# Cross attention on one core: SyncE issues the three k parts of a stack after the values and the first half of the rows

## The chip, the cores and the metric

The kernel runs on one NeuronCore of a Trainium2 chip. The metric is the device time of one execution in microseconds (us). Five engines work side by side: TensorE (PE, with its weight loads shown as PEld), VectorE (DVE), ScalarE (ACT), GpSimd (POOL) and SyncE (SP). SP computes nothing; it issues nearly all DMAs of this kernel, in the order of its program, and it waits on semaphores between them.

## The reference

A cross attention with 16 batches of 256 queries, 256 keys, width 320 and 20 heads of 16. The last 8 keys are 4 "dummy" and 4 "ip" tokens with their own weights, their own softmax and a mask built from boxes:

```python
q = split_heads(x @ w_q)                       # (16, 20, 256, 16)
k, v = split_heads(text @ w_k), split_heads(text @ w_v)       # 248 keys
out_text = softmax(q @ k.T / 4) @ v
k_ip, v_ip = split_heads(ip_h @ w_k_ip), split_heads(ip_h @ w_v_ip)   # 8 keys
out_ip = softmax(q @ k_ip.T / 4 + mask_ip) @ v_ip
out = (out_text + out_ip) @ w_out + b_out + x
```

All of it is float32. The kernel splits operands into high and low parts to keep the accuracy in TensorE's faster float format.

## The kernel before

**First stage** (about the first 210 us): eight groups of two batches each project q, k and v, split q and k into high and low parts, and write them to DRAM (`q_parts`, `k_parts`, `v_rows`).

**Second stage**: 16 batches, one after the other, each with 10 pairs of heads. `batches` runs batches 0 and 1 written out, then a hardware loop of two rounds over six batches (2 to 7, 8 to 13), then 14 and 15. What matters here is how a batch b uses what SP brings:

- A **stack** is what the scores of one batch need: q rows and k rows of all heads, interleaved over the partitions in four kinds of rows. Kinds 0 to 2 are q parts (`load_q`) or k parts (`load_k`), kind 3 of q is the mask (`load_aux`). There are three stacks in turn (w = batch modulo 3). A stack takes seven DMAs of 320 KB, all on the semaphore `stack_loaded[w]`.
- In batch b TensorE computes for each pair p `key_scores(b, p)` (L716, transposed scores that ScalarE turns into `probs` with an exponential, L471) and right behind it `query_scores(b + 1, p)` (L666, scores of the NEXT batch, from which VectorE takes the row maxima, L534 and L536). `values` (L730) and the output projection (L739) follow in between. `query_scores(b + 1, 0)` waits for the whole stack of b + 1, all seven DMAs (L654). So the stack b + 2, which SP issues during batch b, is asked for by the second group of matmuls of batch b + 1.
- **Rows**: the maxima of batch b + 1 go into row 31 of the q stack of b + 1. When VectorE has the maxima of five pairs, it turns them (`turn`, L542) into `row_buf`; SP writes them to DRAM (`store_rows`, L227), waits until they have landed (L229) and reads them back into the stack (`load_rows`, L232). `key_scores(b + 1, 0)` waits for the rows of the first half (h = 0, L712), `key_scores(b + 1, 5)` for those of the second.
- **Values**: `load_values` (L297, L299) brings 660 KB for batch b + 1; it may start once `values` of batch b - 1 are done, that is shortly after batch b begins.

TensorE's order within a batch is fixed by hand, and each wait in it holds everything behind it. So is SP's order, which is the function `batch` of the sync block. In it `scored(t, 0)` waits until key scores of batch b - 1 are done, so that the stack b + 2 may take the place of b - 1; at that point of the program the wait has long been fulfilled.

Of the kernel before, what the change touches and what calls it, by code (L numbers as in the profile page):

```python
# [29 lines left out]
def xattn(nc, x, xT, ctxT, ctx_sp, bbox, wq, wk, wv, wk_ip, wv_ip, wo, bias, grid, kaux, vones, out):  # L30
# [12 lines left out]
    with ctx:  # L43
# [106 lines left out]
        def need(eng, s, value):  # L150
            if not isinstance(value, int) or value > 0:
                eng.wait_ge(s, value)
# [11 lines left out]
        def rows_of(stack, kind):  # L164
            return stack[kind::KINDS, :].rearrange("p (a n) -> p a n", a=PAIRS).bitcast(f32)
# [28 lines left out]
        def _(sp):  # L194
# [30 lines left out]
            def store_rows(b, h):  # L225
                sp.wait_ge(rows_turned, 2 * b + h + 1)
                sp.dma_start(max_rows[h].rearrange("r (t i n) -> i r t n", t=2, i=4),  # L227
                             row_buf[:, h, :].rearrange("p (t n) -> p t n", t=2)).then_inc(rows_stored, 16)
            def load_rows(t, h):  # L229
                sp.wait_ge(rows_stored, 16 * (2 * t.b + h + 1))  # L230
                dst = q_stacks[t.w][2 * DH - 1::2 * DH, h * HALF * S:(h + 1) * HALF * S]
                sp.dma_start(dst.rearrange("p (a n) -> p a n", a=HALF).bitcast(f32),  # L232
                             max_rows[h][0:4 * HALF, :].rearrange("(a x) n -> x a n", x=4)).then_inc(rows_loaded[h], 16)
# [42 lines left out]
            def load_q(t, j):  # L276
                src = q_parts[j // 2, :, bass.ds(t.b * S, S)].rearrange("(a er) n -> er a n", a=PAIRS)
                sp.dma_start(rows_of(q_stacks[t.w], j), src).then_inc(stack_loaded[t.w], 16)  # L278
            def load_aux(t):
                src = aux_rows[bass.ds(t.b, 1), :, :].rearrange("a r n -> (a r) n")  # L280
                sp.dma_start(rows_of(q_stacks[t.w], KINDS - 1),
                             src.unsqueeze(1).broadcast_to([2 * DH, PAIRS, S])).then_inc(stack_loaded[t.w], 16)
            def load_k(t, j):
                src = k_parts[j % 2, :, bass.ds(t.b * KEYS, KEYS)].rearrange("(a er) n -> er a n", a=PAIRS)
                sp.dma_start(rows_of(k_stacks[t.w], j), src).then_inc(stack_loaded[t.w], 16)  # L285
            def load_stack(t):
                for j in range(3):
                    load_q(t, j)
                load_aux(t)
                for j in range(3):  # L290
                    load_k(t, j)
# [4 lines left out]
            def load_values(b, u):  # L296
                sp.dma_start(v_cur[:, u, 0:2, :], v_rows[bass.ds(b, 1), :, :, :].rearrange(  # L297
                    "a k p n -> (a p) k n")).then_inc(v_loaded[u], 16)
                sp.dma_start(v_cur[P - NSP:P, u, 2, :], v_sp_rows[bass.ds(b, 1), :, :].rearrange(  # L299
                    "a p n -> (a p) n")).then_inc(v_loaded[u], 16)  # L300
            def load_residual(b, u):
                sp.dma_start(x_res[:, u, :, :], rows(x[bass.ds(b * S, S), :])).then_inc(xr_loaded[u], 16)
# [12 lines left out]
            def scored(t, p):  # L315
                need(sp, st_ready, PAIRS * t.b + p)
            def batch(t):
                b, u = t.b, t.u
                ahead, next_, first = t.there(2), t.there(1), isinstance(b, int) and b == 0
                if not first:  # L320
                    load_rows(t, 1)
                if t.there(-2):
                    store_out(b - 2)
                load_residual(b, u)
                if ahead:
                    scored(t, 0)
                    load_stack(t.to(2))
                if next_:
                    need(sp, pv_ready, QUADS * b)
                    load_values(b + 1, 1 - u)  # L330
                    store_rows(b + 1, 0)
                    load_rows(t.to(1), 0)
                    store_rows(b + 1, 1)
            def store_out(b):
                need(sp, out_done, OT * (b + 1))
                sp.dma_start(rows(out[bass.ds(b * S, S), :]), out_sb[:, :, :]).then_inc(out_stored, 16)
            batches(sp, batch, tail=False)
            for b in (B - 2, B - 1):
                store_out(b)
# [473 lines left out]
```

## Time and profile before

| | |
|---|---|
| median of 3 runs | 558.0 us (553.15 to 563.45) |
| the profiled execution, device time | 556.4 us |
| its span (first to last instruction) | 554.6 us |
| PE busy, DVE busy, ACT busy | 87%, 69%, 51% of the span |
| second stage, batches 0 to 15 | from 211.8 us to the end |
| data moved | 112.49 MB, mean 203 GB/s |

The span is 1.8 us shorter than the device time of that execution. Matmuls are pipelined and their ends are modelled, so that a busy PE is not PE at its peak; what counts below are the distances between starts.

### The profile page before, as it was taken

The numbers are of one execution on the slowest core, as the hardware profiler recorded it, in microseconds if no ns is written. First come the engines' busy times: TensorE is split into PE (matmuls) and PEld (weight loads), VectorE is DVE, ScalarE is ACT, GpSimd is POOL, SyncE is SP. The second block draws the span as 40 slices with busy tenths as digits, with TensorE's granted clock in tenths as the row PEclk, the third lists the DMA queues.
The fourth block names the chain that finished last, engine by engine and source line by source line (L and its number), as shares of the span: only waits on it lengthen the run. The fifth ranks groups of instructions, "written<-read, shape, count | busy, mean of one in ns | idle before, by whom it ended". The sixth has DMA issues, their size and how long they took to land.

```text
span 554.6 us, 12517 instructions
## 1 busy us (share of the span) xinstructions
PE 481.5 (87%) x4304; PEld 323.7 (58%) x4304; DVE 384.9 (69%) x706; ACT 280.3 (51%) x355; POOL 127.9 (23%) x205
## 2 busy tenths in 40 slices
PE   3979899999999586799799889897987988989985
PEld 2868687887887463455455555554554555555542
DVE  2739425325325256899779989897997999999932
ACT  3633335344344013666556666565664666666671
POOL 6014000000000000432323332331332433332341
PEclk9989999999999787999979999999998999999999
DMA  8978888888788935672681762672754654763211
GB/s 271 362 266 149 259 298 273 309 268 293 272 261 270 345 120 179 200 243 74 204 261 33 247 221 89 234 233 79 235 170 154 219 154 144 245 204 103 72 52 47
DMA packets 94195, 112.49 MB, mean 203 GB/s; under 512 B 14304, under 2 KB 72992, under 8 KB 94144
## 3 DMA queue, kind: packets, MB, share of 16 engines
q1 hardware_dynamic: 93296, 109.89, 60.6%
q0 software_dynamic: 848, 1.90, 1.9%
q8 instruction: 33, 0.54, 0.4%
q14 instruction: 18, 0.15, 0.1%
HBM read 73.17 MB, written 38.63 MB: 202 GB/s over the span
## 4 chain that ended last, share of the span: by engine, by line
PE 48%; DMA 15%; issue 11%; SPq 10%; DVE 9%; ACT 4%; POOL 3%; DVEq 0%; ACTq 0%; POOLq 0%
PE pv L730 10%; DMA max_rows<-row_buf 10%; PE score_t L716 5%; PE pj L739 4%; PE score_q L666 3%; ACT probs L471 3%; SPq L278 3%; PE score_t L625 3%; PE score_t L626 3%; PE score_t L627 3%; SPq L285 2%; PE pj L625 2%; DMA q_stack<-max_rows 2%; PE pj L627 2%; PE pj L626 2%
## 5 line engine op out<-in xcount | busy, mean ns | idle before, releaser
L534 DVE TENSOR_REDUCE max_cols<-score_q 128x4 fp32r<-128x992 f32 x160 | 187.1, 1170 | 46.4 <-PE score_q L666 41.1
L471 ACT ACTIVATE probs<-score_t 128x1024 f32<-128x1024 f32 x160 | 163.4, 1021 | 72.0 <-PE score_t L716 71.9
L730 PE MATMUL pv<-probs,v_cur 128*32 128x256 f32 x1920 | 124.5, 394 | 0.6 <-ACT probs L471 0.6
L387 POOL TENSOR_TENSOR o_turned<-o_turned,inv_cols 128x256 f32<-128x256 f32 x80 | 49.8, 622 | 179.7 <-DVE inv_cols L589 179.7
L716 PE MATMUL score_t<-q_stack,k_stack 64*128 64x256 f32 x440 | 56.5, 335 | 29.4 <-ACT probs L471 17.6
L730 PEld LDWEIGHTS pv<-probs,v_cur 128*32 128x32 f32 x1920 | 55.3, 111 | 41.1 <-issue 4.6
L462 ACT ACTIVATE o_all<-pv 128x512 f32<-128x512 f32 x80 | 47.8, 598 | 60.7 <-PE pv L730 60.7
L716 PEld LDWEIGHTS score_t<-q_stack,k_stack 64*128 64x128 f32 x440 | 33.8, 189 | 74.8 <-ACT probs L471 37.7
L739 PE MATMUL pj<-wo_sb,o_all 128*128 128x320 f32 x192 | 69.0, 468 | 2.9 <-DVE o_all L594 2.2
L381 POOL TENSOR_TENSOR x_all<-x_all,bias_sb 128x640 f32<-128x640 f32 x16 | 24.9, 1554 | 192.5 <-DMA x_all<-in_x 192.5
L586 DVE STREAM_TRANSPOSE o_turned<-o_all 128x512 f32<-128x512 f32 x80 | 56.1, 702 | 11.9 <-ACT o_all L462 11.9
L666 PE MATMUL score_q<-k_stack,q_stack 64*128 64x256 f32 x440 | 47.2, 293 | 12.1 <-DVE max_cols L536 7.0
L513 DVE TENSOR_TENSOR stack<-o_all,stack 128x1024 fp32r<-128x1024 f32 x16 | 19.0, 1222 | 54.3 <-ACT stack L406 54.3
L666 PEld LDWEIGHTS score_q<-k_stack,q_stack 64*128 64x128 f32 x440 | 35.7, 195 | 15.0 <-DVE max_cols L536 6.9
L739 PEld LDWEIGHTS pj<-wo_sb,o_all 128*128 128x128 f32 x192 | 31.1, 188 | 18.7 <-DVE o_all L594 3.9
L392 POOL TENSOR_TENSOR o_all<-o_turned 128x128 f32<-128x128 f32 x80 | 36.7, 459 | 9.3 <-POOL o_turned L387 5.5
L716 PE MATMUL score_t<-stack 64*128 64x256 f32 x200 | 25.2, 330 | 10.6 <-ACT probs L471 7.0
L716 PEld LDWEIGHTS score_t<-stack 64*128 64x128 f32 x200 | 15.0, 184 | 31.3 <-ACT probs L471 16.1
L536 DVE TENSOR_REDUCE max_cols<-score_q 128x4 fp32r<-128x32 f32 x160 | 28.8, 180 | 0.0
L417 ACT ACTIVATE qk_out<-score_t 128x512 fp32r<-128x512 f32 (+1 forms) x24 | 13.9, 593 | 24.8 <-PE score_t L627 14.4
L625 PE MATMUL pj<-stack,wk_hl 128*128 128x512 f32 x32 | 13.8, 430 | 11.4 <-DVE stack L513 11.4
L525 DVE TENSOR_TENSOR qk_out<-score_t,qk_out 128x512 fp32r<-128x512 f32 (+1 forms) x24 | 15.8, 681 | 9.6 <-ACT qk_out L417 9.6
(134 smaller groups left out, 719.5 us busy)
## 6 DMA issues: line engine op xcount, KB each, us to landing
q_stack<-q_parts SPq DMA_DIRECT2D x33, 320.0 KB, 4.5
k_stack<-k_parts SPq DMA_DIRECT2D x33, 320.0 KB, 5.6
v_rows<-v_out SPq DMA_DIRECT2D x32, 320.0 KB, 2.4
v_cur<-v_rows SPq DMA_DIRECT2D x16, 640.0 KB
o_all<-in_ctxT SPq DMA_DIRECT2D x16, 512.0 KB, 5.2
q_parts<-qk_out SPq DMA_DIRECT2D x32, 256.0 KB, 2.5
k_parts<-qk_out SPq DMA_DIRECT2D x32, 248.0 KB, 4.7
x_all<-in_x SPq DMA_DIRECT2D x16, 320.0 KB, 3.3
```

Source lines behind the costliest of these rows:

```text
L387: pool.tensor_tensor(out, out, inv_cols[:, k, :].unsqueeze(2).broadcast_to([P, 2 * S // 32, DH]), ALU.mult).then_inc(scaled, 1)
L392: pool.tensor_tensor(o_norm_t[:, k // 2, :, half:half + DH], out[:, 0:S // 32, :], out[:, S // 32:, :], ALU.add).then_inc(o_added, 1)
L462: nc.scalar.activation(o_raw[:, k, :], pv[:, :], ACT.Copy)\
L471: nc.scalar.activation(probs[:, slot(u, p), :], score_t[:, :], ACT.Exp, scale=SCALE)\
L534: nc.vector.tensor_reduce(out=max_cols[:, h, :, at:at + 4:2].rearrange("p t e -> p e t"), in_=both[:, :, :, 0:TEXT], op=ALU.max, axis=AX.X ...
L536: nc.vector.tensor_reduce(out=max_cols[:, h, :, at + 1:at + 4:2].rearrange("p t e -> p e t"), in_=both[:, :, :, TEXT:KEYS], op=ALU.max, ax ...
L586: nc.vector.transpose(turned_blocks(k), o_raw[:, k, :].rearrange("p (j n) -> p j n", n=32))\
L625: mm(out, w_hi, x_hi_, start=start, stop=False)
L666: last = mm(score_bank(first, p, e)[:, tile * KEYS:(tile + 1) * KEYS], q_cols(w, p, e, tile * P, P), k_cols(w, p, e, 0, KEYS), start=True, ...
L716: last = mm(score_t[:, 512 * e + S * tile:512 * e + S * tile + S], k_cols(t.w, p, e, tile * P, P), q_cols(t.w, p, e, 0, S), start=True, st ...
L730: last = mm(pv[32 * t:32 * t + 32, at:at + S], values_of(u, kind, 4 * k + t), probs[:, slot(u, 2 * k + t // 2), a:a + S], start=kind != 1, ...
L739: last = mm(pj[:, 0:D], o_norm[:, u, c, t * P:t * P + P], wo_sb[:, c, :], start=c == 0, stop=c == OC - 1)
```

## The change

In SP's program of a batch, `load_stack` is taken apart. q and mask of the stack b + 2 keep their place. The three k parts are issued after the values of b + 1, after the store of the first half of the rows and after their load, which itself waits for the landing of the store. The store of the second half stays last. No DMA is added or removed, and no semaphore changes.

```diff
                 if ahead:
                     scored(t, 0)
-                    load_stack(t.to(2))
+                    for j in range(3):
+                        load_q(t.to(2), j)
+                    load_aux(t.to(2))
                 if next_:
                     need(sp, pv_ready, QUADS * b)
                     load_values(b + 1, 1 - u)
                     store_rows(b + 1, 0)
                     load_rows(t.to(1), 0)
+                if ahead:
+                    for j in range(3):
+                        load_k(t.to(2), j)
+                if next_:
                     store_rows(b + 1, 1)
```

## Rows read from the trace of the kernel before

**Rows 1.** The page, the chain that ended last, shares of the span by line

```profile
PE pv L730 10%; DMA max_rows<-row_buf 10%; PE score_t L716 5%; PE pj L739 4%; PE score_q L666 3%; ACT probs L471 3%; SPq L278 3%; PE score_t L625 3%; PE score_t L626 3%; PE score_t L627 3%; SPq L285 2%; PE pj L625 2%; DMA q_stack<-max_rows 2%; PE pj L627 2%; PE pj L626 2%
```

**Rows 2.** Waits of the whole span: us in total, times, longest

```profile
PE score_t L716 <- DMA q_stack<-max_rows: 11.8, 7, 3.2
...
PE score_t L716 <- DMA stack<-max_rows: 1.4, 1, 1.4
```

**Rows 3.** Windows from one batch's first key scores to the next's (batches 3, 4, 5, 6, 10)

```profile
276.00:298.31 22.31, 20.93 (x212) 11.90 (x213) 17.49 (x33) 12.79 (x15) 5.83 (x9) 0.85 0.52 168
298.31:319.04 20.73, 18.10 (x212) 10.69 (x212) 19.64 (x41) 12.69 (x15) 6.93 (x11) 1.00 0.57 182
319.04:338.73 19.69, 18.12 (x212) 10.72 (x213) 17.71 (x35) 12.68 (x15) 6.96 (x11) 1.00 0.58 191
338.73:359.94 21.21, 18.09 (x213) 10.70 (x213) 19.86 (x42) 12.68 (x15) 6.92 (x11) 1.00 0.55 178
...
423.88:445.06 21.18, 19.65 (x213) 11.22 (x213) 17.47 (x33) 12.68 (x15) 6.59 (x11) 0.92 0.54 177
```

The columns are: the window, its length, busy us (and count) of PE, PEld, DVE, ACT and POOL, the granted clock, the busy share of the DMA engines, GB/s.

**Rows 4.** Timeline of PE and PEld where batches 4 and 5 begin: start, us

```profile
298.31 0.51 PE L716 MATMUL score_t<-q_stack,k_stack 64*128 64x256 f32 x4 [0.32 <-ACT probs L471]
...
319.04 0.50 PE L716 MATMUL score_t<-stack 64*128 64x256 f32 x4 [1.36 <-DMA stack<-max_rows]
...
319.27 0.31 PEld L666 LDWEIGHTS score_q<-k_stack,q_stack 64*128 64x128 f32 x4
```

**Rows 5.** Timeline of SP's queue in batch 4

```profile
299.63 0.53 SPq L227 DMA_DIRECT2D max_rows<-row_buf  x1
302.62 0.54 SPq L232 DMA_DIRECT2D q_stack<-max_rows  x1
...
304.52 2.20 SPq L278 DMA_DIRECT2D q_stack<-q_parts  x3
306.91 0.60 SPq L281 DMA_DIRECT2D q_stack<-aux_rows  x1
307.60 2.23 SPq L285 DMA_DIRECT2D k_stack<-k_parts  x3
310.08 0.91 SPq L297 DMA_DIRECT2D v_cur<-v_rows  x1
...
311.62 0.60 SPq L227 DMA_DIRECT2D max_rows<-row_buf  x1
316.87 0.57 SPq L232 DMA_DIRECT2D stack<-max_rows  x1
```

**Rows 6.** Timeline of DVE in the middle of batch 4

```profile
308.61 0.21 DVE L542 STREAM_TRANSPOSE row_buf<-max_cols 128x64 f32<-128x64 f32 x1
```

**Rows 7.** Timeline of SP's queue late in batches 5 and 6

```profile
336.30 0.56 SPq L232 DMA_DIRECT2D q_stack<-max_rows  x1
...
357.78 0.57 SPq L232 DMA_DIRECT2D q_stack<-max_rows  x1
```

**Rows 8.** Windows of 4 us in batch 4 (columns as above)

```profile
304.00:308.00 4.00, 4.00 (x52) 2.43 (x44) 3.84 (x8) 2.54 (x3) 1.64 (x3) 1.00 0.84 249
308.00:312.00 4.00, 3.69 (x50) 2.03 (x42) 3.74 (x9) 2.54 (x3) 2.15 (x4) 1.00 1.02 331
```

**Rows 9.** L293, the mask rows of k for stack 2, one DMA

```profile
DMA to landing us min/median/max: 3.0/3.0/3.0
```

**Rows 10.** L278, third q part of a burst, in batch 13

```profile
L278 SPq DMA_DIRECT2D q_stack<-q_parts x1: 602/602/602, 492.0 to 492.0; - x1
...
DMA to landing us min/median/max: 4.6/4.6/4.6
```

**Rows 11.** L278, third q part of a burst, in batch 1

```profile
L278 SPq DMA_DIRECT2D q_stack<-q_parts x1: 612/612/612, 238.8 to 238.8; - x1
...
DMA to landing us min/median/max: 5.2/5.2/5.2
```

**Rows 12.** Timeline of PE where batches 3, 8 and 10 begin

```profile
276.00 0.50 PE L716 MATMUL score_t<-q_stack,k_stack 64*128 64x256 f32 x4 [3.24 <-DMA q_stack<-max_rows]
...
381.54 0.51 PE L716 MATMUL score_t<-stack 64*128 64x256 f32 x4 [2.24 <-issue]
...
423.88 0.53 PE L716 MATMUL score_t<-q_stack,k_stack 64*128 64x256 f32 x4 [1.90 <-DMA q_stack<-max_rows]
```

## The prediction

> **What bounds the kernel now.** I read the chain first. Beside TensorE's own work its largest entry is a tiny transfer, the store of the row maxima, with 10% of the span [rows 1]. That is a share of the chain and no loss: the chain runs through SP's whole sequence of a batch because, at some batch starts, the rows arrive a little late. How late is in the waits: TensorE idles 13.2 us before L716 for the loaded rows, in 8 batch starts [rows 2]. I then cut the second stage at each batch's first key scores [rows 3]. Batch 4 takes 20.73 us, batch 5 19.69, batch 6 21.21. Batch 4 ends in a wait of 1.36 us and began with one of 0.32 us for ScalarE, which every undisturbed start shows [rows 4]. So 20.73 - (1.36 - 0.32) = 19.69: the batch itself takes 19.7 us, and what is above that is waiting. A late start is followed by an early one, because SP's sequence hangs on VectorE's last turn of rows, which a late start does not delay.
>
> Two batches take longer for another reason. Batch 3 took 22.31 us at a mean granted clock of 0.85, and batch 10 21.18 us at 0.92 [rows 3]; both began after TensorE had waited, 3.24 and 1.90 us, while 2.24 us at batch 8 brought no such fall [rows 12]. Above 19.7 they are 2.6 and 1.5 us.
>
> **What goes.** The row waits: 13.2 us less the 0.3 us that stays at each of the 8 starts is 10.8 us. The slow clock behind two of them: 2.6 + 1.5 = 4.1 us. With neither, this execution's span of 554.6 us would be 554.6 - 10.8 - 4.1 = 539.7 us. That is the floor from which I count.
>
> **Do the rows really come in time?** In batch 4 VectorE has the rows ready at 308.61 + 0.21 = 308.8 us [rows 6], but SP issues their store at 311.62, behind the three k parts (from 307.60 to 310.08) and the values [rows 5]. Without the k parts the store goes out 2.48 us earlier, at 309.1, which is still behind VectorE, so nothing new holds it. It landed at 316.87, when SP goes on to the load. The DMA engines were full from 308 (share 1.02, 331 GB/s) [rows 8], and 960 KB less in front of it at 331 to 360 GB/s is 2.7 to 2.9 us; both ways of counting agree on 2.5 to 2.9. I take 2.5. Counted from the batch's start T, the landing before was T + 18.6 in batch 4 (316.87 - 298.31), T + 19.05 in batch 6 and, with the 1.04 us of its late start added back, T + 18.3 in batch 5 [rows 5, 7], 18.65 in the mean. It becomes T + 16.15. The rows are in the stack about 2.2 us later (319.04 - 316.87 [rows 4, 5]), at T + 18.35, where they are needed at T + 19.7. The row wait is gone with 1.3 us to spare. q, mask, values and the store itself are otherwise as before.
>
> **What comes: the k parts are late.** They used to be issued from T + 9.3 (307.60 - 298.31). Now SP issues them after the landing of the row store, which it waits for, and after the row load, 0.57 us and 0.1 for the step between. The queue they are moved past is SP's alone: values (needed in the third pair, with time to spare), store, wait and load of the rows. Behind them in SP's program stands only the store of the second half, for which VectorE is ready at about T + 20.8; SP is through with the k parts at T + 19, so that costs SP nothing. The transfer of these rows, though, is now behind k data that is still under way, where before it met an empty queue (299.63 to 302.62 [rows 5]). I charge 0.15 us for that to the next batch's sequence, which makes the landing T + 16.3.
> The third k part starts at 16.3 + 0.57 + 0.1 + 2 x 0.7 = T + 18.35 (three in 2.23 us [rows 5]). No row shows a burst of k parts into an empty queue. From below, one DMA of the same shape, alone, lands after 3.0 us [rows 9], and a third one can hardly be quicker, since parts are issued every 0.7 us and 320 KB take 0.97 us at 331 GB/s: 3.0 + 2 x 0.27 = 3.5 us. From above, the third q part of a burst took 4.6 us in batch 13, with residual and output still in front of it, and 5.2 us in batch 1 [rows 10, 11]. I take 4.2, nearer to 4.6 than to 3.5. So the stack is complete at 18.35 + 4.2 = T + 22.55.
> It is asked for 0.23 us after the next batch's start (319.27 against 319.04 [rows 4]), at T + 19.9. **TensorE waits 2.65 us** before `query_scores`, with values, projection and all later key scores queued behind, and ScalarE and VectorE run dry behind it. If that batch had itself waited, this wait moves its end, and the wait at the following start is smaller by the same amount: two neighbouring waits sum to 2.65 us. There are 14 such starts (the stacks 2 to 15), so 7 x 2.65 = 18.6 us.
>
> **The clock.** Each wait of about 2.7 us lies between the 1.90 and 3.24 us that were followed by a fall and above the 2.24 us that was not [rows 12]. I let three of seven have it, at the mean of the two prices, 2.05 us: 6.2 us. Its ends are none and seven times 2.6, 0 to 18 us.
> The Trainium skill (TensorE: Matmul & The Clock Gate, HAM oscillation) describes just this case, a loop in which matmuls wait for a DMA and each wait starts them again at half clock, and prices the throttled time at one half. By that rule each long wait would cost, which is my third case below. The trace agrees on one long wait and disagrees on the 2.24 us one.
>
> **Sum.** 539.7 + 18.6 + 6.2 = 564.5 us of span, + 1.8 us around it = 566.3 us against 556.4. The median shown is 558.0, 1.003 times this execution, so 568 us, 1.8% more.
>
> **The rivals.**
> *Forecast, k late by 2.65 us per two batches*: 568 us, with its own range 559 to 578. Chance 0.58; what a measurement can tell apart here is about 2% (547 to 569 us), and I split this case 0.33 within and 0.25 slower.
> *The k burst is quick*: landing 3.5 us after the third issue and rows 0.3 us earlier give T + 21.55, 1.65 us per two batches: 7 x 1.65 = 11.6 us, and waits that short left the clock alone in batch 5. 539.7 + 11.6 + 1.8 = 553.1, times 1.003 = 555 us. For it: the queue is empty when the burst starts. Against: every burst in the trace took longer. Chance 0.18, within 2%.
> The Trainium skill (DMA: Bandwidth & Descriptors, Anatomy of one DMA) gives about 2 us fixed plus bytes at 436 GB/s for a DMA of GpSimd's path; as an estimate from that page three parts would be in 2.8 us after the third issue, and the whole would be near 550 us. The single DMA of 3.0 us [rows 9] is close to it (2.7), the bursts are not.
> *Dearer on both counts*: the burst takes 5.2 us, the landing of the row store is later (T + 16.8), so the stack is in at T + 24.1 and 4.2 us per two batches, 29 us, and each wait drops the clock, 7 x 2.6 = 18 us: 589 us; halfway to it 579. Chance 0.15, slower.
> *Faster, by one mechanism*: the row store is not held by the data in front of it. In an empty queue it lands after 3.0 us (299.63 to 302.62, when SP goes on [rows 5]). Were that so behind 16 busy engines as well, it would land at 309.1 + 3.0, T + 13.8, the third k part would start at T + 15.85 and be in at T + 20.05, where T + 19.9 is the point from which nothing waits. Then 539.7 + 1 (7 x 0.15) + 1.8 = 542.5, 544 us, 2.5% faster. For it: the store moves only 32 KB. Against: it took 5.25 us from 311.62 in full engines, and at 309.1 some 3540 - 960 - 1350 = 1230 KB (what batch 4 issued by then less what had moved at 249 and 331 GB/s [rows 8]) are still ahead of it, 3.7 us. Chance 0.09, faster.
>
> **Range and chances.** 549 to 582 leaves out the fast rival and the worst of the dear one. Faster 0.09, within 2% 0.51, slower 0.40.
>
> **What would show it.** After: no wait of L716 for loaded rows; instead PE and PEld at L666 wait for the DMA of k_stack<-k_parts, some 18 us in total, every second batch start, longest near 3 us; L227 of the first half at T + 10.9 and L232 at T + 16.3; batch windows of 22.3 and 19.7 us by turns, some at a clock below 1.00. I am wrong if the third k part lands under 1.7 us after its issue or the row store lands by T + 13.7; or if the waits at L666 spread evenly and stay short, in which case the clock term falls away (562 us).

## The result and the profile after

| | before | changed |
|---|---|---|
| median device time | 558.2 us (4 runs) | 575.1 us (571.9 to 580.4, 4 runs) |
| ratio | | 1.034, 95% interval 1.023 to 1.046 |
| profiled execution: span | 554.6 us | 570.1 us |

The change makes the kernel 3.4% slower. The ratio, here and below, is formed from runs that lie within 1.5% of the fastest one of the same kernel. The profiled execution is the fastest of the four runs of the changed kernel (571.9 us of device time), so its account below is on the mild side. Everything behind the edit stands 6 lines further down in the file: L716 is now L722, L666 is L672, L730 is L736, L471 is L477; L227, L232 and L285 keep their numbers.

The chain that ended last, shares by line, from the page of the changed kernel (answers to [rows 1]):

```profile
PE pv L736 10%; DMA max_rows<-row_buf 9%; DMA k_stack<-k_parts 5%; DMA stack<-k_parts 4%; PE score_q L672 4%; PE score_t L722 4%; ACT probs L477 3%; DVE max_cols L540 3%; PE score_t L631 3%; SPq L285 3%; PE score_t L632 3%; PE score_t L633 3%; PE pj L745 3%; PE pj L631 2%; PE pj L633 2%
```

The row store is still there, but two new links have come in, the k parts, with 9% together. The waits from 222 us to the end (us in total, times, longest; to be set against [rows 2]):

```profile
PE score_q L672 <- DMA k_stack<-k_parts: 9.9, 5, 2.9
...
PE score_q L672 <- DMA stack<-k_parts: 6.6, 5, 2.9
```

No wait of L722 for rows is left. In its place TensorE waits 16.5 us for k parts, in 10 places. SP's queue in batch 4, which begins at 293.68 us (answers to [rows 5]; the third k part's landing below it, from the view of its line):

```profile
300.25 2.19 SPq L278 DMA_DIRECT2D q_stack<-q_parts  x3
302.63 0.60 SPq L281 DMA_DIRECT2D q_stack<-aux_rows  x1
303.48 0.41 SPq L297 DMA_DIRECT2D v_cur<-v_rows  x1
...
304.76 0.59 SPq L227 DMA_DIRECT2D max_rows<-row_buf  x1
310.36 0.57 SPq L232 DMA_DIRECT2D stack<-max_rows  x1
311.04 2.11 SPq L285 DMA_DIRECT2D k_stack<-k_parts  x3
```

```profile
L285 SPq DMA_DIRECT2D k_stack<-k_parts x1: 606/606/606, 312.5 to 312.5; - x1
...
DMA to landing us min/median/max: 4.1/4.1/4.1
```

With T for the start of the batch, the store goes out at T + 11.1, SP goes on at T + 16.7, the third k part starts at T + 18.9 and is in 4.1 us later, at 316.6. In the next batch, which waits for it, the same store goes out later and takes less (SP's queue in batch 5, which begins at 313.91):

```profile
328.62 0.59 SPq L227 DMA_DIRECT2D max_rows<-row_buf  x1
331.01 0.56 SPq L232 DMA_DIRECT2D q_stack<-max_rows  x1
```

It leaves at T + 14.7, because VectorE gets the scores and so has the maxima later, and SP goes on 2.4 us behind it, at T + 17.1, against 5.6 us in batch 4, where the stack parts and values were issued shortly before the store.

TensorE takes the third part of batch 4 up at 316.79, in the timeline of PE where batches 5, 7 and 14 ask for the stack and where batch 8 begins:

```profile
316.79 0.76 PE L672 MATMUL score_q<-k_stack,q_stack 64*128 64x256 f32 x4 [2.38 <-DMA k_stack<-k_parts]
...
361.16 0.76 PE L672 MATMUL score_q<-stack 64*128 64x256 f32 x4 [2.91 <-DMA stack<-k_parts]
...
385.08 0.78 PE L722 MATMUL score_t<-stack 64*128 64x256 f32 x4 [3.26 <-issue]
...
515.92 0.80 PE L672 MATMUL score_q<-k_stack,q_stack 64*128 64x256 f32 x4 [2.88 <-DMA k_stack<-k_parts]
```

Windows from one batch's first key scores to the next's, for batches 3, 4, 5, 6, 7, 8, 10, 11 and 14 (columns and meaning as in [rows 3]):

```profile
271.42:293.68 22.26, 18.42 (x213) 10.78 (x214) 18.74 (x38) 12.68 (x15) 6.91 (x11) 1.00 0.62 198
293.68:313.91 20.23, 18.34 (x213) 10.76 (x214) 18.71 (x38) 12.68 (x15) 6.90 (x11) 1.00 0.50 154
313.91:337.79 23.88, 19.96 (x212) 11.29 (x213) 18.71 (x38) 12.68 (x15) 6.88 (x11) 0.93 0.57 185
337.79:357.74 19.95, 18.09 (x212) 10.72 (x213) 18.64 (x38) 12.68 (x15) 6.91 (x11) 1.00 0.50 152
357.74:385.08 27.34, 19.93 (x212) 11.26 (x213) 19.97 (x42) 12.68 (x15) 7.95 (x13) 0.94 0.52 167
385.08:406.36 21.28, 19.69 (x212) 11.39 (x213) 17.45 (x33) 12.68 (x15) 5.88 (x9) 0.92 0.56 177
...
427.28:450.61 23.33, 19.87 (x212) 11.28 (x213) 18.71 (x38) 12.68 (x15) 6.88 (x11) 0.93 0.54 170
450.61:470.32 19.71, 18.12 (x213) 10.73 (x214) 18.63 (x38) 12.68 (x15) 6.90 (x11) 1.00 0.53 172
...
512.53:539.00 26.47, 22.26 (x212) 12.39 (x213) 18.77 (x38) 12.78 (x15) 6.92 (x11) 0.81 0.27 86
```

The last batch, from its first key scores to the end of the span:

```profile
539.00:570.10 31.10, 23.13 (x208) 11.87 (x208) 10.76 (x27) 13.27 (x16) 9.00 (x15) 0.88 0.14 45
```

Three things are to be seen. A batch without a wait still takes 19.7 to 20 us (batches 6 and 11). Batches with a wait and at full clock take that plus the wait (batch 3: 22.3). Batches with a clock below 1.00 take more: batch 5 is 23.88 - 19.69 = 4.2 us over, of which 2.6 are the wait as the weight load shows it (0.2 more than the matmul's 2.38), so 1.6 us are the clock. The last batch took 29.43 us at a clock of 0.99 in the kernel before, and takes 31.10 us at 0.88 here.

### The profile page after: what moved, and what is told of

The parts are those of the page before. It is cut to its first block, busy times and chain, and to the rows that moved or that the text cites. A ratio compares the mean times of both kernels' runs of the same rounds, so it can differ in the third digit from the quotient of the medians.

```text
span 570.1 us, 12517 instructions
## 1 busy us (share of the span) xinstructions
PE 491.6 (86%) x4304; PEld 328.0 (58%) x4304; DVE 385.4 (68%) x706; ACT 280.4 (49%) x355; POOL 127.4 (22%) x205
## 4 chain that ended last, share of the span: by engine, by line
PE 45%; DMA 20%; issue 11%; DVE 10%; SPq 7%; ACT 5%; POOL 2%; ACTq 0%; DVEq 0%; POOLq 0%
PE pv L736 10%; DMA max_rows<-row_buf 9%; DMA k_stack<-k_parts 5%; DMA stack<-k_parts 4%; PE score_q L672 4%; PE score_t L722 4%; ACT probs L477 3%; DVE max_cols L540 3%; PE score_t L631 3%; SPq L285 3%; PE score_t L632 3%; PE score_t L633 3%; PE pj L745 3%; PE pj L631 2%; PE pj L633 2%
## 5 line engine op out<-in xcount | busy, mean ns | idle before, releaser
L477 ACT ACTIVATE probs<-score_t 128x1024 f32<-128x1024 f32 x160 | 163.3, 1021 | 62.8 <-PE score_t L722 62.7
L736 PE MATMUL pv<-probs,v_cur 128*32 128x256 f32 x1920 | 129.0, 404 | 0.6 <-ACT probs L477 0.6
L736 PEld LDWEIGHTS pv<-probs,v_cur 128*32 128x32 f32 x1920 | 56.5, 114 | 43.7 <-issue 9.0
L722 PE MATMUL score_t<-q_stack,k_stack 64*128 64x256 f32 x440 | 55.8, 331 | 20.9 <-ACT probs L477 20.8
L745 PE MATMUL pj<-wo_sb,o_all 128*128 128x320 f32 x192 | 70.5, 477 | 2.7 <-DVE o_all L600 1.9
L722 PEld LDWEIGHTS score_t<-q_stack,k_stack 64*128 64x128 f32 x440 | 33.6, 187 | 65.6 <-ACT probs L477 35.9
L672 PE MATMUL score_q<-k_stack,q_stack 64*128 64x256 f32 x440 | 48.3, 299 | 20.6 <-DMA k_stack<-k_parts 13.6
L592 DVE STREAM_TRANSPOSE o_turned<-o_all 128x512 f32<-128x512 f32 x80 | 56.1, 702 | 11.8 <-ACT o_all L468 11.8
L672 PEld LDWEIGHTS score_q<-k_stack,q_stack 64*128 64x128 f32 x440 | 36.0, 197 | 24.7 <-issue 10.7
L745 PEld LDWEIGHTS pj<-wo_sb,o_all 128*128 128x128 f32 x192 | 32.0, 193 | 18.6 <-DVE o_all L600 2.9
L722 PE MATMUL score_t<-stack 64*128 64x256 f32 x200 | 26.1, 340 | 10.4 <-ACT probs L477 7.1
L722 PEld LDWEIGHTS score_t<-stack 64*128 64x128 f32 x200 | 15.6, 192 | 32.6 <-issue 17.1
L672 PE MATMUL score_q<-stack 64*128 64x256 f32 x200 | 20.9, 288 | 6.6 <-DMA stack<-k_parts 6.6
```

The costliest lines, as they stand in the source:

```text
L477: nc.scalar.activation(probs[:, slot(u, p), :], score_t[:, :], ACT.Exp, scale=SCALE)\
L592: nc.vector.transpose(turned_blocks(k), o_raw[:, k, :].rearrange("p (j n) -> p j n", n=32))\
L672: last = mm(score_bank(first, p, e)[:, tile * KEYS:(tile + 1) * KEYS], q_cols(w, p, e, tile * P, P), k_cols(w, p, e, 0, KEYS), start=True, ...
L722: last = mm(score_t[:, 512 * e + S * tile:512 * e + S * tile + S], k_cols(t.w, p, e, tile * P, P), q_cols(t.w, p, e, 0, S), start=True, st ...
L736: last = mm(pv[32 * t:32 * t + 32, at:at + S], values_of(u, kind, 4 * k + t), probs[:, slot(u, 2 * k + t // 2), a:a + S], start=kind != 1, ...
L745: last = mm(pj[:, 0:D], o_norm[:, u, c, t * P:t * P + P], wo_sb[:, c, :], start=c == 0, stop=c == OC - 1)
```

## The experiments

All but the last are variants of SP's order (or, three of them, of TensorE's first pair), timed in three rounds beside the kernel before on the same chip. "Ratio" is to the kernel before. T is again the start of a batch. Where a ratio's interval reaches over 0.98 or 1.02, it is not shown that the difference is 2% or more.

**1. k parts ahead of SP's wait, `k_before_wait`.** Only the row load is moved, behind the k parts:

```diff
                     store_rows(b + 1, 0)
-                    load_rows(t.to(1), 0)
                 if ahead:
                     for j in range(3):
                         load_k(t.to(2), j)
                 if next_:
+                    load_rows(t.to(1), 0)
                     store_rows(b + 1, 1)
```

> SP issues q, mask, values, the row store, then the three k parts, and only then waits for the landing of the store and loads the rows. Theory (the k parts are late because SP sits in the wait for the landing before it issues them): they go out at T + 11.3 instead of T + 17, the stack is in by T + 18.5, the row store keeps the landing it has in the changed kernel, and neither wait is left: a ratio to the kernel before of 0.97 to 0.98 (543 to 547 us) and no waits of L672 for k parts. Rival (what hurts is that k stands behind values and store, whose bytes fill the engines): the k wait stays at half or more, ratio 1.00 to 1.02. Second rival (the row load is now held behind 960 KB of k data): waits of key scores for rows instead, about as many as before, ratio 0.99 to 1.00.

Ratio 0.977 (0.971 to 0.984), 547.6 us. SP's queue in batch 4, which begins at 292.81:

```profile
303.42 0.59 SPq L227 DMA_DIRECT2D max_rows<-row_buf  x1
304.12 2.83 SPq L285 DMA_DIRECT2D k_stack<-k_parts  x3
309.62 0.57 SPq L232 DMA_DIRECT2D stack<-max_rows  x1
```

The k parts go out at T + 11.3 instead of T + 17.4, the row store still lands so that SP goes on at T + 16.8, and the third k part is in at T + 19.5 (5.9 us after its issue; I had expected T + 18.5), 0.4 us before it is asked for. There is no wait of L672 after 222 us at all. What is left are small waits for rows (same view as above, 222 us to the end):

```profile
PE score_t L722 <- DMA q_stack<-max_rows: 1.6, 3, 0.6
PE score_t L722 <- DMA stack<-max_rows: 0.6, 1, 0.6
```

The theory holds, both rivals fall. The place of one statement, on this or that side of one semaphore wait, is worth 1.034 - 0.977 = 5.7% of the kernel.

**2. k parts behind the values only, `k_after_values`.** SP: q, mask, values, k, store, load.

> SP issues q, mask, values, k parts, then the row store and its load: against the kernel before only values and k parts are swapped. Theory: k parts behind 660 KB of values are not late (in by about T + 18), the row store goes out as late as before, so everything is as before: ratio 0.995 to 1.005, row waits of about 13 us, none for k. Rival (k behind the values is itself the loss): k waits appear, ratio 1.01 to 1.02.

The four runs took 555.4, 557.9, 563.9 and 567.1 us, beside a median of 560.3 (556.9 to 561.8) for the kernel before: no difference that can be measured. In its profile the row waits are 13.3 and 2.7 us, against 11.8 and 1.4 before, and no k wait appears. So 660 KB of values ahead of the k parts make no k wait, though with less margin than I had expected: the third part takes 6.7 us in batch 4 and is in at T + 18.9.

**3. The store as early as VectorE allows, `store_k_load_values`.** SP: q, mask, store, k, load, values.

> SP issues q and mask, waits for the turned rows and stores them, then k parts, row load, values. Theory: the store has only q and mask in front of it, lands near T + 14, k parts are out by T + 13.5 and in by T + 18, the values arrive by T + 20 and are asked for at T + 23: no waits at all at the batch starts, ratio 0.97 to 0.98. If it is faster than the order with values in front, the row landing still mattered there; if the same, both are at the floor of 19.7 us a batch. Rival (the values become late, or SP's wait for VectorE delays k): waits at pv or at L672, ratio 0.99 or more.

Ratio 0.974 (0.968 to 0.979), 544.6 us, span 540.2 us. No wait for rows or k parts after 222 us. The windows of batches 4 and 5:

```profile
289.59:309.26 19.67, 18.08 (x212) 10.71 (x213) 18.62 (x38) 12.68 (x15) 6.92 (x11) 1.00 0.61 191
309.26:328.96 19.70, 18.13 (x214) 10.72 (x214) 18.64 (x38) 12.68 (x15) 6.92 (x11) 1.00 0.60 192
```

That is the floor: 19.7 us a batch, and a span 0.5 us from the 539.7 us from which the prediction counted. That the two agree so closely is in part chance. This execution had a fall of the clock behind the loop's turn (1.5 us) and a longer turn (3.0 us against 2.24), which the floor does not contain, and it reached batch 1 at 230.5 us, where the kernel before, less its wait for rows, would have done so at 232.0. It and experiment 5 have the lowest times; the intervals of experiments 1, 3 and 5 overlap.

**4. TensorE kept at work, `after_fill` and `after_fill8`.** Matmuls whose result is overwritten stand ahead of the wait for the stack in the changed kernel, 13 or 8 of them:

```diff
+                fillers = not (isinstance(b, int) and b < 2)
                 first = isinstance(b, int) and b == 0
+                if p == 0 and fillers:
+                    pe.wait_ge(max_done, PAIRS * b - 1)
+                    for n in range(13):
+                        mm(score_bank(False, 0, 0)[:, 0:KEYS], wq_hi[0:HEAD, 0, 0:P],
+                           x_hi[0:HEAD, 0, 0:KEYS], start=True, stop=True)
                 if p == 0:
                     pe.wait_ge(stack_loaded[w], 112 * (t.r + 1))
```

> The changed kernel with 13 idle-filling matmuls (64x256, result thrown away, about 1.4 us in all) ahead of the wait for the stack in batches whose stack is late; the output is the same. Theory of two terms (waits of 18 us, and 10 us of slow clock that follow them): the fillers take up the waits and keep TensorE at work, so the time of the waits stays and the slow clock goes: span 560 to 563 us, ratio 1.005 to 1.015, granted clock 1.00 in nearly every batch. Rival (the slow clock costs little, the waits are the whole loss): span as in the changed kernel or longer, 570 to 580 us, since the fillers add to batches that do not wait.

Ratio 1.022 (1.016 to 1.028), 571.2 us, span 568.5 us: neither side's number. A batch without a wait took 21.2 us instead of 19.7, so the fillers cost 1.5 us a batch, 14 x 1.5 = 21 us, more than I had set. The waits for k parts fell to 1.3 us, and apart from the loop's turn (386 to 394 us) and the last microseconds there was no slow clock after 222 us. So they removed 15 us of waits and the slow clock behind them and put in 21 us of work. The interval of the ratio touches that of the changed kernel (1.023 to 1.046), so the total does not settle it, and I ran fewer of them.

> As the run with 13 filling matmuls, but with 8, about 1.0 us per batch, less than the mean wait. Theory: fillers and waits together stay at 18 to 19 us, every single wait is below 1.9 us, so the slow clock behind the late k parts goes (10 us in the changed kernel, of which 1.6 behind the loop): span 561 to 565 us, ratio 1.005 to 1.015. Rival (the clock costs nothing of its own): span as in the changed kernel, 570 us, ratio 1.02 to 1.03.

Ratio 1.031 (1.019 to 1.043), 573.2 us, span 569.0 us. This expectation missed. Fillers (a batch without a wait takes 20.6 us, so 14 x 0.9) and waits (4.5 us) sum to 17 us, about as expected, but the slow clock did not go. PE's timeline where batches 4, 6 and 10 ask for the stack, and windows of 2 us behind them (the clock is the third column from the right):

```profile
296.94 0.58 PE L678 MATMUL score_q<-stack 64*128 64x256 f32 x4 [1.08 <-DMA stack<-k_parts]
...
341.78 0.80 PE L678 MATMUL score_q<-k_stack,q_stack 64*128 64x256 f32 x4 [1.88 <-DMA k_stack<-k_parts]
...
432.88 0.50 PE L678 MATMUL score_q<-stack 64*128 64x256 f32 x4 [0.75 <-DMA stack<-k_parts]
```

```profile
298.00:300.00 2.00, 2.00 (x24) 0.68 (x16) 1.25 (x3) 0.00 (x0) 0.00 (x0) 0.50 0.05 14
...
342.00:344.00 2.00, 2.00 (x20) 1.07 (x24) 1.38 (x3) 0.00 (x0) 0.00 (x0) 0.50 0.00 0
...
434.00:436.00 2.00, 2.00 (x20) 0.78 (x12) 1.11 (x3) 0.23 (x1) 0.00 (x0) 0.50 0.04 11
```

With 8 fillers waits of 1.08, 1.88 and 0.75 us are left in these batches, and the clock falls to half behind each; 13 fillers leave no wait above 0.6 us, and it does not. What the three falls cost is seen in the stretch from batch 1's first key scores to batch 15's, first with 13 fillers, then with 8:

```profile
232.77:539.13 306.36, 278.93 (x3150) 173.22 (x3151) 261.72 (x518) 177.60 (x210) 96.92 (x154) 0.99 0.52 165
```

```profile
231.74:537.22 305.48, 275.50 (x3082) 166.54 (x3082) 261.66 (x518) 177.85 (x210) 96.77 (x154) 0.97 0.53 165
```

Against 8 fillers, 13 are some 8.2 us more work (14 x 0.6) and save 3.2 us of waits, and the loop's turn was 0.4 us longer, so the stretch should be 5.4 us longer. It is 0.9 us longer. The three falls behind k waits were therefore worth about 4.5 us, 1.5 us each, as in the changed kernel. The slow clock is a cost of its own, and it does not need a long wait. The medians alone (571.2 and 573.2 us, with overlapping intervals of the ratio) would not show it.

**5. The opposite edit, `store_before_values`.** The stack stays whole and first, as before; only values move behind the row store, and ahead of the row load.

```diff
                 if next_:
+                    store_rows(b + 1, 0)
                     need(sp, pv_ready, QUADS * b)
                     load_values(b + 1, 1 - u)
-                    store_rows(b + 1, 0)
                     load_rows(t.to(1), 0)
```

> The stack is issued whole as in the kernel before; only the values move, behind the row store and ahead of the row load. Theory (the rows were late by about 1 us, through what is in front of their store): the store goes out 1.5 us earlier with 660 KB less in front, lands at about T + 16.9 and is loaded by T + 19.1; k parts are in by T + 18 as before; no waits, ratio 0.97 to 0.98, equal to the best order so far. Rival (only taking the k parts from in front helps the rows): row waits of 5 us or more stay, ratio 0.985 to 1.0.

Ratio 0.979 (0.969 to 0.988), 544.8 us. The row waits fell from 13.2 us to 2.3 us (whole span):

```profile
PE score_t L716 <- DMA q_stack<-max_rows: 1.5, 2, 1.0
PE score_t L716 <- DMA stack<-max_rows: 0.8, 1, 0.8
```

SP's queue in batch 4, which begins at 290.65:

```profile
302.23 0.59 SPq L227 DMA_DIRECT2D max_rows<-row_buf  x1
303.09 2.04 SPq L297 DMA_DIRECT2D v_cur<-v_rows  x1
...
308.44 0.59 SPq L232 DMA_DIRECT2D stack<-max_rows  x1
```

The rows did not need the k parts out of their way. The landing came at T + 17.8, not at the T + 16.9 I had worked out (I take it that the values behind the store share the engines with it, which no run here separates), but 0.9 us against the T + 18.65 of before is nearly all that was missing.

**6. One k part late, `one_k_late`.** The first two k parts stay ahead of the values; the third is issued behind the row load.

> As the changed kernel, but only the third k part is issued behind the landing of the row store; the first two keep their place. Theory (what counts is when the LAST k part is issued, and that is the landing of the store plus its own 3 to 3.5 us): the store now lands later, at T + 17.8, the part is in at T + 21.5 to 22, so the waits of L672 stay at 1.6 to 2.1 us per two batches, 11 to 15 us in all, few falls of the clock: ratio 0.995 to 1.01. Rival (the loss goes by the late bytes): a third of the waits, 5 to 6 us, and ratio 0.98 to 0.985.

Ratio 1.024 (1.014 to 1.033), 570.3 us; the profiled execution was quicker, 562.6 us of span. The waits after 222 us:

```profile
PE score_q L673 <- DMA stack<-k_parts: 5.9, 5, 1.5
PE score_t L723 <- DMA q_stack<-max_rows: 5.5, 4, 1.9
PE score_q L673 <- DMA k_stack<-k_parts: 3.9, 3, 1.6
```

The k waits are 9.8 us, not the third part (5 to 6) of the rival, though below the 11 to 15 I gave. A single part behind the landing takes 3.3 to 5.3 us, median 3.5, where the third of a burst takes 4.2. What I had left out is that with two k parts back in front of the store the row waits are back too, 5.5 us, so both prices are paid. That does not explain all of it: the profiled execution, 564.5 us, is only 1.1% above the median of the kernel before (558.3), and the others, 568.2 to 570.8 us, had lower granted clocks (0.947 to 0.954 against 0.964). More falls of the clock are likely the rest, but no trace shows them.

**7. The stack asked for later, `after_values_first`.** In TensorE's first pair of the changed kernel, `values` stands ahead of `query_scores`.

> The changed kernel, with TensorE's order at the first pair turned: values of the batch before (1.5 us of matmuls) stand ahead of the query scores that wait for the stack. Theory (it is that one wait that costs, by how early it is asked): the stack is asked for 1.3 to 1.5 us later, two neighbouring waits sum to 0 us instead of 2.6, ratio 0.975 to 0.985. Rival (VectorE now gets its first maxima 1.3 us later in each batch and cannot make that up): the batch itself grows to 20.5 us or more, ratio 0.995 to 1.01.

Ratio 1.010 (1.005 to 1.015), 563.1 us: the rival's range. Waits for k parts are 7.3 us (4.8 and 2.5) instead of 16.5, so the ask does count. But the batch grew. VectorE's turns of the second half, which end a batch's maxima, in the timeline of DVE:

```profile
316.25 0.19 DVE L548 STREAM_TRANSPOSE row_buf<-max_cols 128x64 f32<-128x64 f32 x1
...
336.57 0.18 DVE L548 STREAM_TRANSPOSE row_buf<-max_cols 128x64 f32<-128x64 f32 x1
```

20.32 us for a batch with no wait of TensorE for a DMA, against 19.7, over 14 batches some 8 us. VectorE is busy 18.6 us of 19.7 (the windows of experiment 3). In batch 5 here (315.15 to 335.47) it waits 2.0 us for query scores, the longest wait 1.1 us, against 1.1 us and 0.4 us in batch 4 of experiment 3. That fits a late first block that it cannot make up; no run separates this from other causes. The theory of no wait at all missed too: the k parts are still behind the row store, which with the later scores goes out at T + 11.4 in batch 11 instead of T + 10.5 in the changed kernel.

**8. The wait kept, the bytes in front taken away, `store_load_k_values`.** As the changed kernel (k behind SP's wait), but the values last.

> As the changed kernel, the k parts behind SP's wait for the landing of the row store, but the values are moved behind them. Theory (k is late by the time of that landing, which is set by the bytes in front of the store): with only q and mask in front the store goes out at T + 10.6 and lands at T + 14, the third k part is issued at T + 16 and in by T + 20 to 20.4, where it is asked for at T + 19.9: two neighbouring waits sum to 0.1 to 0.5 us, ratio 0.975 to 0.985. Rival (issuing k behind the wait is the loss whatever stands in front): ratio above 1.01.

Ratio 1.009 (1.003 to 1.015), 563.5 us. Between the two: the k waits are 10.0 us instead of 0.7 to 3.5 (seven times 0.1 to 0.5). SP's queue in batch 3, and the landing of the third k part of that batch:

```profile
285.87 0.59 SPq L227 DMA_DIRECT2D max_rows<-row_buf  x1
288.26 0.57 SPq L232 DMA_DIRECT2D q_stack<-max_rows  x1
288.94 2.09 SPq L285 DMA_DIRECT2D stack<-k_parts  x3
291.28 0.40 SPq L297 DMA_DIRECT2D v_cur<-v_rows  x1
```

```profile
L285 SPq DMA_DIRECT2D stack<-k_parts x1: 602/602/602, 290.4 to 290.4; - x1
...
DMA to landing us min/median/max: 7.2/7.2/7.2
```

The landing of the row store came about as early as worked out (T + 14.5; 2.4 us after its issue, against 5.6 in batch 4 of the changed kernel), so the wait itself is short when little is in front of it. But the third k part, with the values issued 0.9 us after it, took 7.2 us here, and 4.5 to 7.2 us over the 14 bursts, median 5.4; in the changed kernel, where nothing large follows, the 14 took 4.0 to 6.1 us, median 4.2. That data issued BEHIND a transfer lengthens it I had not counted. The 1.2 us make two neighbouring waits 1.2 us longer, 7 x 1.2 = 8.4 us, about the miss.

**9. The mask late as well, `mask_and_k_late`.**

> As the changed kernel, but the mask rows too are issued behind the landing, ahead of the k parts. Theory: the store has 320 KB less in front and lands 0.8 us earlier, the last k part is issued one part (0.7 us) later behind it and finds a queue fuller by 0.3 us: the stack is complete within 0.3 us of where it is in the changed kernel, waits 16 to 21 us, ratio 1.02 to 1.045, no clear difference to the changed kernel. Rival (the loss goes by the late bytes, a third more): waits of 24 us and ratio 1.045 to 1.06.

Ratio 1.027 (1.023 to 1.032), 574.3 us; the changed kernel beside it has 1.032 (1.026 to 1.037). A third more late bytes cost nothing more. Its profiled execution took 583.2 us, where the other three took 573.6 to 574.5, so I read no waits from it.

**10. The changed kernel again, `changed_again`.**

> The changed kernel as it is, for a second profile on this chip. If waits and clock are as accounted: waits of L672 for k parts 15 to 20 us, 4 to 6 falls of the clock, span 568 to 577 us, ratio 1.02 to 1.045.

Ratio 1.032 (1.026 to 1.037), 575.8 us, span 575.5 us. The waits after 222 us:

```profile
PE score_q L672 <- DMA k_stack<-k_parts: 10.7, 4, 3.8
PE score_q L672 <- DMA stack<-k_parts: 8.2, 4, 3.5
```

18.9 us in 8 places (and one wait for rows, of 0.7 us), and seven stretches of half clock between 222 and 540 us, six of them behind a k wait and one at the loop's turn.

## Why the prediction was right

**What goes.** Right. No wait for rows is left in the profile of the changed kernel, 0.7 us in the second one, and the floor of 539.7 us was met by a kernel without waits (540.2 us, in part by chance, see experiment 3). The cause I gave for the late rows, what stands in front of their store, is shown by experiments 1, 3 and 5, which each take something else away, and by experiment 2, which takes nothing away and keeps the waits.

**What comes.** Right in mechanism and in size. The row store landed at T + 16.7 in batch 4 (forecast T + 16.3), the third k part took 4.1 us (forecast 4.2, median of 14 bursts 4.2), and the waits alternated up to batch 8; behind it batches 9 and 10, and 12 and 13, shared one between them. Over the 14 batch starts they lengthened the batches by 18.5 us (the ten weight loads that waited, in batches 1, 3, 4, 5, 7, 9, 10, 12, 13 and 14: 0.97, 2.40, 0.49, 2.58, 3.11, 1.16, 2.07, 1.71, 0.93 and 3.08) against 18.6. One step held for a reason that I did not give. I had the landing at T + 16.3 in every batch. In a batch that has waited the store goes out 1 to 5 us later than the T + 10.5 of one that has not, since VectorE's maxima are later, but mostly lands quicker (batch 5: 2.4 us against 5.6), so that the landing stays between T + 14.5 and T + 17.6 in batches 1 to 13, 16.2 in the mean. Experiment 1 shows that it is SP's wait for the landing that makes them late, and experiment 2 that the values in front do not. Experiment 9 shows that it does not go by the late bytes.

**The clock.** The term that was mis-sized. I gave 6.2 us for three falls. The profiled execution had four behind k waits (batches 5, 7, 10 and 14) and one behind the loop's turn at batch 8. By the windows they cost 1.6 + 1.6 + 1.6 + 3.7 and 1.6, together 10.1 us; in batch 14 the clock stayed low for most of 514 to 526 us. So the price of one fall was right (2.1 us in the mean of the four, 2.05 in the forecast), their number too low, and none was set for the loop's turn, nor for the last batch, which lost another 1.7 us. The second profile had seven, with a span 5.4 us longer. My choice hung on waits between 1.90 and 3.24 us; experiment 4 shows that 0.75 us can be followed by a fall, and batch 3 of the changed kernel that 2.20 us need not be. So the length of a wait alone does not decide it, and three of seven was a guess.

The case in the Trainium skill (TensorE: Matmul & The Clock Gate, HAM oscillation) has waits for a DMA that are longer than the matmuls between them; here some 20 us of work stand between waits of at most 3.8 us, so it is not just this case, as I had written. If each k wait had brought a fall there would have been ten; there were four here, and six behind eight waits in the second profile.

**The sum.** 539.7 + 18.5 + 10.1 = 568.3; the turn of the loop took 3.26 instead of 2.24 us, + 1.0; the last batch 31.10 instead of 29.43 us, + 1.7; and batch 1 began at 231.06 us instead of 232.0, - 0.9. That is 570.1, the measured span. Against the forecast span of 564.5 us it is 3.9 us of clock, 1.0 of the loop, 1.7 of the last batch, less 0.1 of waits and 0.9 of the start. The profiled run was the fastest; the median, 575.1 us, is 3.2 us further up, and the granted clock of the other three runs is lower (0.944 to 0.949 against 0.952). The profile of experiment 10, of a run of 577.3 us, shows more falls of the clock. So the forecast of 568 us (1.8% slower) is 7 us short of the median (3.4% slower), and what the record shows of that lies in the clock, the loop and the last batch, not in the waits.

**The rivals.** The quick k burst did not come: the third part took 4.0 to 6.1 us in the 14 bursts, median 4.2, and never the 3.5 us of that rival. The fast rival (the store not held by what is in front) is refuted by the landing: 5.6 us behind q, mask and values in batch 4, 2.4 us in experiment 8 and in batch 5, where little was still under way. The time came out between my forecast and the dear rival's halfway mark of 579, for that rival's reason of the clock, not for its slower landings.

## What to carry to other kernels

In this kernel the order of a DMA queue's program has two prices: what a transfer stands behind, and what its issuer waits for first. Moving independent loads behind a semaphore wait of the issuer is the dear one; moving them ahead of the wait, behind the issue of the urgent small store, leaves 2.2 us of waits for rows (experiment 1). Giving the small store room in this way, or by moving the values behind it (experiment 5), makes the kernel 2.1 to 2.3% faster. Before giving a late transfer room, work out by how little it is late (here some 1.5 us per two batches, 10.8 us in all) and pay for it with the load that has the most slack, here the values, not with one asked for at the very next batch start.

## What the runs showed of the hardware

- The clock fell to half behind waits of TensorE as short as 0.75 us in an otherwise busy stretch, and did not behind others of 2.2 us; in the changed kernel each fall cost 1.6 to 3.7 us of the batch. Where 13 fillers left no wait above 0.6 us, it did not fall in these batches.
- A DMA can be lengthened by one issued after it on the same queue: the third k part took 4.2 us in the median of 14 with nothing large behind it, and 5.4 us with 660 KB of values issued 0.9 us later (experiment 8). A single part, with nothing behind it, took 3.5 us (experiment 6).
- A 32 KB store from one queue lands 2.4 us after its issue in an idle queue and 5.6 us behind stack parts and values, so small size buys no precedence.
- At the turn of the hardware loop (batch 7 to 8) TensorE idled 2.1 to 4.1 us in these profiles, with nothing in the trace that it waited for.
